# Nine TensorE products that nobody reads are taken out of a transformer tower

## The chip, the cores and the metric

One Trainium2 chip, of which the kernel uses one core, so nothing here goes between cores. A core has five engines that run their own lists of instructions side by side and wait for each other by semaphores: TensorE (PE: matrix products and transposes, written into eight banks of PSUM), VectorE (DVE), ScalarE (ACT), GpSimd (POOL) and SyncE (SP, which issues most DMAs). The metric is the time of one execution on the device in microseconds (us); smaller is better.

## The reference, cut to what matters

64 images are cut into 36 patches of 768 values each, embedded to 256 channels, and two more tokens are set in front. One attention-like layer and one feed-forward layer with 32 experts follow.

```
h = tokens(x) @ W_lin + b_lin (+ class token, positions)       # 64 x 38 x 256
h = h + attn(layernorm(h))     # up, 4-tap conv, q/k/v by blocks, gates,
                               # decayed scores, head norm, down
n = layernorm(h)
shared = silu(n @ gw) * (n @ uw) @ dw
e = argmax(n @ gate_w); s = sigmoid(max(n @ gate_w))
routed = silu(s*n @ G[e]) * (s*n @ U[e]) @ D[e]                # one of 32 experts
out = h + shared + routed
```

## The kernel before, in words

The work has two phases. In the first, eight groups of eight images (304 tokens, in three tiles of 114, 114 and 76 rows) go through everything but the experts. In the second the 32 experts are applied to the tokens that chose them, with weights of 1.5 MB for each expert read from memory.

The first phase is a software pipeline, written out by hand. `pipeline(pe, step)` (L1641) calls `step(e, f, a, m)` eight times: e is the group being embedded, f the group in the first layer norm, the products `up` and the convolution, a the group in attention, m the group in the second layer norm, the routing and the shared feed-forward. In the first steps a and m are None, and the list is short: this is the fill. After the eight steps the lists of the last groups are written out one after the other (L1643 to L1731): this is the drain. Each engine has such a list of its own. TensorE takes its list in order; where a step calls `pe.wait_ge`, everything behind it on TensorE waits too.

Names that the change and the prediction touch:

- `stream(bank, moving, times)` (L1345 to L1348) multiplies the identity by 512 columns of weights that lie in SBUF and writes them to a whole bank. It has no wait and increments no semaphore, and the next user of the bank starts it anew. It is called in six places for nine products in all.
- Fill, group 0, step 2: `h_rows_of` (L1364) transposes the tokens to rows, ACT copies them out (L505), DVE takes the statistics (L868, L872), POOL the reciprocal root (L442, L444), DVE normalises (`xn`, L878), and `to_columns` (L1381) transposes back. ACT and DVE split the result in a high and a low part (L505, L884), and the first of eight `up` products starts (L1390; each `up(f, k)` is six products and six records). `stream(ab[3], lin_w, 4)` stands ahead of `to_columns`, `stream(ab[3], lin_w, 1)` behind it.
- Between weight preparations: `merge_weights` (L1314 to L1321) multiplies small weight matrices, most with 8 columns. `turn_up` (L1331) transposes the `up` weights; DVE copies the two banks out (L831, semaphore `s_prep`); `mixed_gate_weights` (L1340) waits for `s_prep` at 20, which is the second copy, and makes 16 products of 8 columns. `stream(ab[3], lin_w, 1)` stands between `turn_up` and `mixed_gate_weights`. Then come `q_of` (L1416), `h_rows_of` and `scores` (L1455).
- Drain, last group in attention: ACT makes the decay factors (`cw`, L604), DVE weighs them (L950), and `heads(a, j)` (L1490) waits for tile j of them. `stream(fb[1], sd_w, 1)` stands ahead of `heads(a, 0)`. Behind the heads DVE makes the norm (L968 to L977), statistics (L984 to L999) and, after them in its list, `expert_act` (L1117), on which the second half of `gate_up(m, 1)` waits.
- Drain, last group in the shared layer: `ffn_rows` (L1364), `stream`, `to_columns` (L1381), `stream`, `route` (L1529 and L1532, which waits for the low part, L1060), `gate_up(m, 0)`. The second phase can start its products only behind this list (first ones at L2253).

Of the kernel before, what the change touches and what calls it, by code (L numbers as in the profile page):

```python
# [58 lines left out]
def groups_phase(nc, block, patches, w_lin, pos, cols, w_up, conv, chan, wq, wk, wv, wvt, w_gates, b_gates,  # L59
# [4 lines left out]
    fb, ab, mb = banks[0:2], banks[2:6], banks[6:8]  # L64

    with ExitStack() as ctx:
        def sb(name, shape, dt=f32):
            return ctx.enter_context(nc.sbuf_tensor(name, shape, dt))
# [21 lines left out]
        ident = sort.ident  # L90
# [5 lines left out]
        lin_w = sort.lin_w  # L96
# [4 lines left out]
        sd_w = sb("sd_w", [128, KI, D])  # L101
# [1205 lines left out]
        def _(pe):  # L1307
# [34 lines left out]
                last.then_inc(s_prep_mm, 1)  # L1342


            def stream(bank, moving, times):  # L1345
                for _ in range(times):
                    pe.matmul(bank[:, :], ident[:], moving[:, 0:2, :].rearrange("p k d -> p (k d)"),
                              start=True, stop=True)  # L1348

            def embed(f, c):  # L1350
                if c == 0:
                    pe.wait_ge(s_patch, 16 * f.n + 16)
                wait(pe, s_sz, KI * f.n - 1 + c)
                for k in range(KF):
                    last = pe.matmul(fb[c][:, 0:GS * N], lin_w[:, k, c * 128:(c + 1) * 128],  # L1355
                                     patch[:, k, :], start=(k == 0), stop=(k == KF - 1))
                last.then_inc(s_emb_mm, 1)
# [10 lines left out]
            def h_rows_of(f):  # L1368
                if f.n == 0:
                    pe.wait_ge(s_const, CONSTS)  # L1370
                pe.wait_ge(s_ht, KD * f.n + KD)
                to_rows(fb, h_t[:].rearrange("p c s t -> p c (s t)"), s_h_mm)

            def to_columns(dst, src, ready, n, done):

                for c in range(KD):
                    for j in range(NT):
                        if c == 0:
                            pe.wait_ge(ready, NT * n + j + 1)
                        rows = height(j)  # L1380
                        last = pe.transpose(dst[c][:, columns(j)], src[0:rows, j, c * 128:(c + 1) * 128],  # L1381
                                            ident[0:rows, 0:rows])
                    last.then_inc(done, 1)
# [11 lines left out]
            def up(f, k):  # L1395
                if f.n == 0:
                    pe.wait_ge(s_prep, 7 if k < KI else 8)
                if k < 2:
                    pe.wait_ge(s_xnl, KD * f.n + KD)
                elif k < 2 + KI:  # L1400
                    pe.wait_ge(s_xm, KI * f.n + k - 1)
                else:
                    pe.wait_ge(s_sz, KI * f.n + k - KI - 1)
                split_product(fb[k % 2][:, 0:GT], (up_hi, up_lo), (xn_hi, xn_lo), k * 128).then_inc(s_up_mm, 1)


            def q_of(a, heads_at):
                pe.wait_ge(s_xact, KI * a.n + KI)
                if a.n == 0:
                    pe.wait_ge(s_prep, 12)  # L1410
                for h in heads_at:
                    if h < 2:
                        wait(pe, s_att, KD * (a.n - 1) + h + 1)
                    else:
                        wait(pe, s_h2, 2 * a.n)
                    pe.matmul(ab[h][:, 0:GT], score_w[:, h], x_act[:, a.p, h, :],  # L1416
                              start=True, stop=True).then_inc(s_q_mm, 1)
# [4 lines left out]
            def v_of(a, j):  # L1422
                if a.n == 0:
                    pe.wait_ge(s_prep, 18)
                pe.wait_ge(s_ct, NT * a.n + j + 1)
                for h in range(NH):
                    last = pe.matmul(ab[j][0:height(j), h * 128:(h + 1) * 128], xm_tile(a, h, j), v_w[:, h],
                                     start=True, stop=True)
                last.then_inc(s_v_mm, 1)

            def mixed_gates(f):

                if f.n == 0:
                    bank = mb[0]
                    pe.wait_ge(s_prep, 22)
                else:
                    bank = fb[0]
                    pe.wait_ge(s_sz, KI * f.n + 1)
                for j in range(NT):
                    tile = columns(j)  # L1440
                    dst = bank[0:height(j), GT + 16 * j:GT + 16 * (j + 1)]
                    for c in range(KD):
                        pe.matmul(dst, xn_hi[:, c, tile], g_w[:, c], start=(c == 0), stop=False)
                    for c in range(KD):
                        last = pe.matmul(dst[:, 0:2 * NH], xn_lo[:, c, tile], g_w[:, c, 0:2 * NH],
                                         start=False, stop=(c == KD - 1))
                last.then_inc(s_gm_mm, 1)

            def scores(a, j):

                n, w = height(j), height(j) + 2 * NH
                if j == 0:
                    pe.wait_ge(s_q, NH * a.n + NH)
                for h in range(NH):
                    last = pe.matmul(ab[j][0:n, h * w:(h + 1) * w], x_act[:, a.p, h, columns(j)],  # L1455
                                     q_t[:, h, j, 0:w], start=True, stop=True)
                last.then_inc(s_c_mm, 1)

            def f_sums(a):
                pe.wait_ge(s_logf, a.n + 1)  # L1460
                pe.matmul(ab[3][0:R, 0:NT * NH], tri[:], logf[:].rearrange("p j h -> p (j h)"),
                          start=True, stop=True).then_inc(s_f_mm, 1)
# [113 lines left out]
            def ffn_rows(m):  # L1576
                pe.wait_ge(s_ffn, KD * m.n + KD)
                to_rows(mb, ffn_t, s_ft_mm)

            def step(e, f, a, m):  # L1580
                if a: q_of(a, range(1, NH))
                if f: h_rows_of(f)
                if a:
                    scores(a, 0)
                    scores(a, 1)
                    scores(a, 2)
                    if a.n == 0: mixed_gates(a)
                    v_of(a, 0)
                    v_of(a, 1)
                if f and f.n == 0: stream(ab[3], lin_w, 4)  # L1590
                if f: to_columns(fb, xn, s_xn, f.n, s_xnt_mm)
                if f and f.n == 0: stream(ab[3], lin_w, 1)
                if a: v_of(a, 2)
                if m: to_columns(mb, xn2, s_xn2, m.n, s_xn2t_mm)
                if f: up(f, 0)
                if a: f_sums(a)
                if f:
                    up(f, 1)
                    up(f, 2)
                if a: gates_t(a)  # L1600
                if f: up(f, 3)
                if f and f.n == 0: merge_weights()
                if m: route(m)
                if a:
                    tops_t(a)
                    decay(a, 0)
                    decay(a, 1)
                    decay(a, 2)
                if f: up(f, 4)
                if m: gate_up(m, 0)  # L1610
                if a:
                    heads(a, 0)
                    heads(a, 1)
                if a and a.n == 0:
                    heads(a, 2)
                if f: up(f, 5)
                if a and a.n > 0:
                    heads(a, 2)
                if m: gate_up(m, 1)
                if f:  # L1620
                    if f.n > 0: mixed_gates(f)
                    up(f, 6)
                if m:
                    ranks(m)
                    gate_up(m, 2)
                if m: gate_up(m, 3)
                if f: up(f, 7)
                if m: shared_down(m)
                if e: embed(e, 0)
                if m: ffn_rows(m)  # L1630
                if a: heads_t(a)
                if e: embed(e, 1)
                if f and f.n == 0:
                    turn_up()
                    stream(ab[3], lin_w, 1)
                    mixed_gate_weights()
                if a: down(a)
                if f: q_of(f, range(0, 1))
                if a: att_rows(a)

            pipeline(pe, step)  # L1641

            f, a, m = last, next_last, near  # L1643
# [54 lines left out]
            decay(a, 1)  # L1698
            route(m)
            decay(a, 2)  # L1700
            stream(fb[1], sd_w, 1)
            heads(a, 0)
            heads(a, 1)
            gate_up(m, 0)
# [10 lines left out]
            ffn_rows(m)  # L1715

            m = last
            stream(ab[1], sd_w, 1)
            to_columns(fb, xn2, s_xn2, m.n, s_xn2t_mm)
            stream(ab[1], sd_w, 1)  # L1720
            route(m)
            gate_up(m, 0)
            ranks(m)
# [649 lines left out]
```

## Time and profile before

| | us |
|---|---|
| median of 3 runs | 653.28 |
| lowest and highest | 651.33 and 653.66 |
| the profiled execution, own time | 654.7 |
| its span, first to last instruction | 652.9 |
| PE busy in the span | 607.6 (93%) |
| DVE busy | 429.5 (66%) |
| ACT busy | 375.2 (57%) |
| POOL busy | 197.4 (30%) |
| mean granted clock of TensorE | 0.988 of full speed |

The profile is one execution. Its times are from the start of the span. An engine is busy while it executes; a PE that is busy may still run at either of two clocks, 1.2 or 2.4 GHz, and the profile has the granted clock as a share of full speed. A product on fp32 data is two records of TensorE (the nine products are 18 records). Ends of products are modelled; their starts are measured. The chain of waits starts at the instruction that ended last and goes back, at each step, to what released it.

### The profile page before, as it was taken

The page shows a single profiled execution, that of the slowest core. Times are in us where ns is not written, and L with a number is a line of the kernel's source. Part 1 is how long each engine was busy: PE and PEld are TensorE (multiplying, and loading weights), DVE is VectorE, ACT ScalarE, POOL GpSimd, SP SyncE. Part 2 cuts the span into 40 slices and gives each one's busy share as a digit, 9 for nine tenths or more (in the row PEclk, how much of TensorE's full clock was granted, in tenths as well). Part 3 has the DMA queues.
Part 4 walks back from the last instruction along what each step waited for, and adds up shares of the span by engine and source line. Part 5 has one row for each costly group of instructions (what it writes and reads, how often), then busy time and mean ns, then how long its engine had stood idle before and what let it go on. Part 6 is the DMA issues. An engine that isn't in the chain of part 4 may idle for free.

```text
span 652.9 us, 10636 instructions
## 1 busy us (share of the span) xinstructions
PE 607.6 (93%) x3615; PEld 510.1 (78%) x3615; DVE 429.5 (66%) x1338; ACT 375.2 (57%) x839; POOL 197.4 (30%) x226
## 2 busy tenths in 40 slices
PE   4899899999998998999999998988999999999995
PEld 3688778878878878878878977766788888888884
DVE  1644785865856865866765866675876777776672
ACT  1328668449439529539538758243666666666661
POOL 5100110231232133133033233353256662232451
PEclk9999899999999999999998999899999999999999
DMA  8339410030030030030010011185999999999960
GB/s 291 132 85 369 122 56 1 20 94 21 20 95 21 20 94 21 19 95 21 8 51 20 2 37 37 35 303 169 392 391 378 379 348 350 373 369 404 343 214 23
DMA packets 44597, 101.56 MB, mean 156 GB/s; under 512 B 9295, under 2 KB 30589, under 8 KB 39672
## 3 DMA queue, kind: packets, MB, share of 16 engines
q1 hardware_dynamic: 35280, 89.07, 38.1%
q0 software_dynamic: 7696, 8.49, 4.7%
q10 hardware_dynamic: 1560, 3.23, 1.5%
q8 instruction: 32, 0.52, 0.4%
q14 instruction: 29, 0.24, 0.1%
HBM read 80.17 MB, written 23.32 MB: 159 GB/s over the span
## 4 chain that ended last, share of the span: by engine, by line
PE 71%; ACT 14%; DVE 8%; issue 2%; POOL 1%; DMA 1%; SPq 0%; DVEq 0%; ACTq 0%; POOLq 0%
PE bank L2253 16%; PE bank L1390 11%; PE bank L2272 9%; PE bank L1355 8%; PE bank L1512 4%; PE bank L1490 3%; PE bank L1455 3%; PE bank L2261 2%; PE bank L1416 2%; PE bank L1572 2%; PE bank L1364 2%; ACT v L505 2%; ACT hst L581 2%; ACT L596 1%; ACT L592 1%
## 5 line engine op out<-in xcount | busy, mean ns | idle before, releaser
L456 POOL TENSOR_TENSOR rstd_h<-var_h,minus_half 114x4 f32<-114x4 f32 (+1 forms) x24 | 24.3, 1014 | 173.3 <-DVE var_h L999 173.3
L2077 POOL DMA_INDIRECT out<-rows,bg x32 | 37.6, 1175 | 82.4 <-DVE rows L2143 81.1
L1355 PE MATMUL bank<-patch,lin_w 128*128 128x288 f32 x192 | 52.6, 428 | 8.7 <-DMA col_t<-cols 7.9
L2253 PE MATMUL bank<-w_hi,x_hi 128*128 128x512 f32 x148 | 56.5, 463 | 2.7 <-DVE x_lo L2155 2.7
L1355 PEld LDWEIGHTS bank<-patch,lin_w 128*128 128x128 f32 x192 | 37.4, 201 | 20.6 <-DMA col_t<-cols 7.9
L898 DVE SCALAR_TENSOR_TENSOR y<-xm,conv_t,y 128x296 f32<-128x296 f32 (+2 forms) x96 | 43.7, 512 | 6.2 <-ACT xm L505 6.2
L2253 PE MATMUL bank<-w_lo,x_hi 128*128 128x512 f32 x148 | 46.3, 394 | 0.0
L2253 PE MATMUL bank<-w_hi,x_lo 128*128 128x512 f32 x148 | 46.2, 393 | 0.0
L2179 DVE TENSOR_TENSOR act_e<-silu_e,bank 128x512 f32<-128x512 f32 x37 | 25.5, 688 | 31.0 <-PE bank L2253 30.3
L2149 DVE TENSOR_TENSOR w_lo<-wts,w_hi 128x1024 fp32r<-128x1024 f32 x36 | 43.1, 1217 | 0.5 <-ACT w_hi L2201 0.5
L2228 ACT ACTIVATE silu_e<-bank 128x512 f32<-128x512 f32 x37 | 22.1, 598 | 35.2 <-PE bank L2253 35.2
L1390 PE MATMUL bank<-xn_hi,up_hi 128*128 128x304 f32 x128 | 33.7, 346 | 6.0 <-ACT xm L505 4.9
L1841 POOL DMA_INDIRECT b_zone_dram<-base_rows,spot x24 | 31.1, 1295 | 26.9 <-DVE base_rows L1125 20.9
L505 ACT ACTIVATE att_t<-bank 128x304 f32<-128x304 f32 x15 | 6.3, 423 | 54.1 <-PE bank L1512 53.4
L2201 ACT ACTIVATE w_hi<-wts 128x1024 fp32r<-128x1024 f32 x36 | 36.8, 1049 | 0.0
L1841 POOL DMA_INDIRECT x_zone_dram<-xs_rows,spot x24 | 30.2, 1259 | 21.1 <-DVE spot L1103 9.0
L2196 ACT ACTIVATE x_hi<-bank 128x256 fp32r<-128x256 f32 x37 | 14.2, 383 | 38.9 <-PE bank L2242 28.1
L2143 DVE SCALAR_TENSOR_TENSOR rows<-bank,bg 128x256 f32<-128x256 f32 x37 | 15.7, 424 | 31.2 <-PE bank L2272 19.3
L1572 PE MATMUL bank<-act_t,sd_w 128*128 128x304 f32 x128 | 35.0, 424 | 1.2 <-DVE act_t L1117 1.2
L1390 PE MATMUL bank<-xn_hi,sgu_hi 128*128 128x304 f32 x128 | 31.6, 329 | 3.4 <-DVE act_t L1117 2.9
L1512 PE MATMUL bank<-hst,down_w 128*128 128x304 f32 x128 | 34.1, 420 | 0.1
L2272 PE MATMUL bank<-wts_down,act_et 128*128 128x256 f32 x144 | 34.1, 379 | 0.0
(261 smaller groups left out, 1658.8 us busy)
## 6 DMA issues: line engine op xcount, KB each, us to landing
wts<-w_exp SPq DMA_DIRECT2D x18, 1024.0 KB
x_act<-w_exp SPq DMA_DIRECT2D x10, 1024.0 KB
silu_z<-w_exp SPq DMA_DIRECT2D x9, 1024.0 KB
wts_down<-w_exp SPq DMA_DIRECT2D x18, 512.0 KB
patch<-patches SPq DMA_DIRECT2D x8, 864.0 KB, 6.0
down_w<-w_exp SPq DMA_DIRECT2D x10, 512.0 KB
lin_w<-w_exp SPq DMA_DIRECT2D x9, 512.0 KB
b_zone_dram<-act_t SPq DMA_DIRECT2D x1, 4160.0 KB, 28.4
```

The costliest lines, as they stand in the source:

```text
L898: dve.scalar_tensor_tensor(y[:, k, :, lag:], xm[:, f.p, k, :, 0:S - lag], w, y[:, k, :, lag:], ALU.mult, ALU.add).then_inc(s_conv, 1)
L1355: last = pe.matmul(fb[c][:, 0:GS * N], lin_w[:, k, c * 128:(c + 1) * 128], patch[:, k, :], start=(k == 0), stop=(k == KF - 1))
L1390: last = pe.matmul(dst, weights[w][:, c, at:at + 128], x[part][:, c, :], start=(n == 0), stop=(n == 3 * KD - 1))
L1512: last = pe.matmul(ab[c][:, 0:GT], down_w[:, k, c * 128:(c + 1) * 128], hst[:, k, :], start=(k == 0), stop=(k == KI - 1))
L1572: last = pe.matmul(mb[c][:, 0:GT], sd_w[:, k, c * 128:(c + 1) * 128], act_t[:, k, :], start=(k == 0), stop=(k == KI - 1))
L1841: pool.indirect_dma_start(zone, bass.IndirectOffsetOnAxis(ap=self.spot[0:n, t:t + 1], axis=0), rows[0:n, j, :], None, bounds_check=E * SLO ...
L2077: pool.indirect_dma_start(out, bass.IndirectOffsetOnAxis(ap=rows_at, axis=0), rows[:, k % 4, :], None, bounds_check=T - 1, oob_is_err=Fals ...
L2149: dve.tensor_tensor(w_lo[:, k % 2, u, :], wts[k % 4][:, u * KD * I:(u + 1) * KD * I], w_hi[:, k % 2, u, :].bitcast(f32), ALU.subtract).the ...
L2179: dve.tensor_tensor(act_e[:, e, :], silu_e[:, e, :], banks[3 + 2 * e][:, :], ALU.mult).then_inc(s_ae, 1)
L2201: act.activation(w_hi[:, k % 2, u, :], wts[k % 4][:, u * KD * I:(u + 1) * KD * I], ACT.Copy).then_inc(s_w_hi, 1)
L2253: last = pe.matmul(banks[2 + 2 * e + u][:, :], x[:, e, c * SLOT:(c + 1) * SLOT], w[:, e, u, c * I:(c + 1) * I], start=(n == 0), stop=(n == ...
L2272: last = pe.matmul(banks[6 + k % 2][:, 0:D], act_et[:, k % 2, c, :], wts_down[k % 4][:, c * D:(c + 1) * D], start=(c == 0), stop=(c == KI ...
```

## The change

All six calls of `stream` and the function itself are taken out. Nothing else is moved; the waits and the order of all other instructions stay.

```
-            def stream(bank, moving, times):
-                for _ in range(times):
-                    pe.matmul(bank[:, :], ident[:], moving[:, 0:2, :].rearrange("p k d -> p (k d)"),
-                              start=True, stop=True)
-
...
                     v_of(a, 0)
                     v_of(a, 1)
-                if f and f.n == 0: stream(ab[3], lin_w, 4)
                 if f: to_columns(fb, xn, s_xn, f.n, s_xnt_mm)
-                if f and f.n == 0: stream(ab[3], lin_w, 1)
                 if a: v_of(a, 2)
...
                 if f and f.n == 0:
                     turn_up()
-                    stream(ab[3], lin_w, 1)
                     mixed_gate_weights()
...
             route(m)
             decay(a, 2)
-            stream(fb[1], sd_w, 1)
             heads(a, 0)
...
             m = last
-            stream(ab[1], sd_w, 1)
             to_columns(fb, xn2, s_xn2, m.n, s_xn2t_mm)
-            stream(ab[1], sd_w, 1)
             route(m)
```

## Rows read from the trace of the kernel before

**Rows 1.** The page: span, engines' busy time, and granted clock in 40 slices.

```profile
span 652.9 us, 10636 instructions
...
PE 607.6 (93%) x3615; PEld 510.1 (78%) x3615; DVE 429.5 (66%) x1338; ACT 375.2 (57%) x839; POOL 197.4 (30%) x226
...
PEclk9999899999999999999998999899999999999999
```

**Rows 2.** The removed line by itself: ns min/median/max, first and last start in us.

```profile
L1347 PE MATMUL bank<-lin_w,ident x12: 592/592/644, 17.3 to 44.8; 128*128 128x512 f32 x12
...
L1347 PE MATMUL bank<-sd_w,ident x6: 592/594/676, 399.5 to 429.5; 128*128 128x512 f32 x6
```

**Rows 3.** The chain of waits: start us, length us, what.

```profile
7.93 8.10 PE bank L1355 x24
...
21.46 0.43 DVE xn L878
...
26.53 1.91 PE bank L1390 x12
...
31.91 4.99 PE bank L1390 x24
36.90 5.83 PE bank L1355 x24
...
44.47 0.91 PE bank L1347 x2
...
432.10 1.93 PE bank L1390 x12
...
436.95 3.65 PE bank L1390 x24
```

**Rows 4.** Timeline, first layer norm of the fill: start, length, idle before <-releaser.

```profile
17.33 3.60 PE L1347 MATMUL bank<-lin_w,ident 128*128 128x512 f32 x8
...
22.96 1.06 PE L1347 MATMUL bank<-lin_w,ident 128*128 128x512 f32 x2
24.35 0.52 PE L1390 MATMUL bank<-xn_hi,up_hi 128*128 128x304 f32 x2 [0.33 <-DVE xn_lo L884]
```

**Rows 5.** Timeline behind `turn_up`.

```profile
44.50 0.69 DVE L831 COPY x_act<-bank 128x512 f32<-128x512 f32 x1 [0.20 <-PE bank L1331]
45.25 1.95 PE L1340 MATMUL bank<-gm_w,x_act 128*128 128x8 f32 x16
```

**Rows 6.** Timeline, heads of the last group.

```profile
399.48 1.10 PE L1347 MATMUL bank<-sd_w,ident 128*128 128x512 f32 x2
399.82 0.63 DVE L950 TENSOR_TENSOR cw<-c_t,cw 114x456 f32<-114x456 f32 x1
...
400.42 1.91 PE L1490 MATMUL bank<-v,cw 114*114 114x128 f32 x16
...
403.20 0.16 DVE L968 COPY norm<-bank 114x4 f32<-114x4 f32 x1 [0.66 <-PE bank L1490]
```

**Rows 7.** Timeline, second layer norm of the last group.

```profile
426.52 1.02 PE L1347 MATMUL bank<-sd_w,ident 128*128 128x512 f32 x2
...
428.00 1.21 PE L1381 MATMUL bank<-ident,xn 114*128 114x114 f32 x6 [0.45 <-DVE xn L1054]
...
429.05 1.06 PE L1347 MATMUL bank<-sd_w,ident 128*128 128x512 f32 x2
...
430.35 0.39 PE L1529 MATMUL bank<-route_w,xn_hi 128*114 128x64 f32 x2 [0.24 <-DVE xn_lo L1060]
```

**Rows 8.** TensorE by stretch: length, PE busy (records), granted clock, DMA share, GB/s.

```profile
29.00:32.00 3.00, 3.00 (x29) 1.00 0.02 5
32.50:35.90 3.40, 3.40 (x16) 0.50 0.00 0
...
404.50:407.90 3.40, 1.24 (x10) 1.00 0.01 4
...
425.30:432.10 6.80, 5.06 (x28) 1.00 0.95 376
```

More of the change, by code:

```diff
@@ L1342, in mixed_gate_weights @@
                 last.then_inc(s_prep_mm, 1)
[L1345 to L1348, printed above, removed]
             def embed(f, c):
@@ L1589, in step @@
                     v_of(a, 1)
-                if f and f.n == 0: stream(ab[3], lin_w, 4)
                 if f: to_columns(fb, xn, s_xn, f.n, s_xnt_mm)
-                if f and f.n == 0: stream(ab[3], lin_w, 1)
                 if a: v_of(a, 2)
@@ L1634, in step @@
                     turn_up()
-                    stream(ab[3], lin_w, 1)
                     mixed_gate_weights()
@@ L1700, in _ @@
             decay(a, 2)
-            stream(fb[1], sd_w, 1)
             heads(a, 0)
@@ L1717, in _ @@
             m = last
-            stream(ab[1], sd_w, 1)
             to_columns(fb, xn2, s_xn2, m.n, s_xn2t_mm)
-            stream(ab[1], sd_w, 1)
             route(m)
```

## The prediction

> **What bounds the kernel now.** The page comes first. PE is busy 607.6 us of a span of 652.9 us, the next engine, DVE, 429.5 us [rows 1]: TensorE sets the pace. The row of granted clock shows four slices at 8 among the 9s [rows 1]: the clock is full nearly always and falls a few times for a moment. Next I looked at the removed line by itself: 12 records in the fill and 6 in the drain, 592 ns of modelled length each [rows 2], but two of them start to start with their neighbours take less: eight take 3.60 us [rows 4], 0.45 us for one, so a product of two records costs TensorE 0.9 us. Nine cost 8.1 us of its time. The chain of waits then says how much of this lies on the path, and the timeline what released the instruction behind each one. The last view is busy time and granted clock by stretch, since the nine products can do one thing besides costing time: keep the clock up.
>
> **What the removal gives back, place by place.**
>
> Layer norm of the fill, five products. The eight records at 17.33 end at 20.93, and the transposes behind them wait for DVE's xn, which starts at 21.46 [rows 3, 4]. The single product at 22.96 ends at 24.02, and the next instruction, at 24.35, was released by DVE xn_lo after an idle 0.33 us [rows 4]. Both lie in waits: 0.0 us.
>
> Behind `turn_up`, one product. The chain has it on the path with 0.91 us [rows 3], which looks like a gain. But `mixed_gate_weights` waits for the second copy of DVE, 44.50 + 0.69 = 45.19, and it starts at 45.25 [rows 5]. The copy is late next, at the same moment: 0.0 us, at most the 0.13 us by which the chain puts the end of the product at 45.38.
>
> Heads of the last group, one product, 399.48, or 0.94 us of TensorE between the last decay product and 400.42. `heads(a, 0)` could start at about 399.6, `heads(a, 1)` needs DVE's second weighing, 399.82 + 0.63 = 400.45, and is reached at about 400.5: no new wait. Who is late next is DVE: its norm at 403.20 idled 0.66 us for the heads [rows 6], and before that DVE had no gap. The chain runs from there through DVE to the next products, so the gain is 0.66 us at most of the 0.94; between 0 and 0.94 I take 0.6 us.
>
> Second layer norm of the last group, two products. 426.52 + 1.02 = 427.54, and the transposes start at 428.00, released by xn; 429.05 + 1.06 = 430.11, and `route` starts at 430.35, released by xn_lo [rows 7]. 0.0 us.
>
> So of 8.1 us of TensorE only 0.6 us come back. No semaphore, DMA or other engine's list is touched, and no wait is added.
>
> **What the clock takes.** Rows 8 have the key. From 29 to 32 PE is busy 3.00 of 3.00 us, but with products of 8 columns (29 records), and then the clock is at 0.50 (1.2 of 2.4 GHz) from 32.5 to 35.9. From 404.5 to 407.9 PE is busy only 1.24 us, waiting for DVE, and the next fall follows. From 425.3 to 432.1 the clock stays full, though the real work in it is 12 transposes and the small products of `route`; 1.02 + 1.06 us of its 5.06 busy us are the four wide records [rows 7, 8]. So the clock falls after a stretch in which few columns go through TensorE, by idling or by tiny products alike, and the nine products stand in just such stretches.
>
> The price of a fall, from rows at either level: 24 records of `up` take 4.99 us where most of them run low, and 24 of the same shape 3.65 us at full clock [rows 3]: 1.34 us. The other bound is a start from a cold engine: the first 24 records of the embedding take 8.10 us, the same 24 later 5.83 us: 2.27 us [rows 3] (the page prints a full clock there; the length of the records says otherwise). A low stretch of 3.4 us at half speed can cost at most 1.7 us; the cold start costs more because it lasts until enough dense work has gone through. After an idle engine I go by the second row, after a busy one by the first.
>
> Fill, layer norm. Without the five products PE has six transposes between 17.3 and 24.35. The clock is low when `up` starts: between 1.34 and 2.27 us, nearest to the cold start, 1.9 us. The 24 records of the four `up` run from 24.35 to 28.44 = 4.09 us where dense ones take 3.65, so 0.4 us is swallowed by waits for ACT. The transposes on the path run low too, +0.2 us (estimate: six in about 1 us, paced half by DVE). Against this stands the fall at 32.5: with `up` late, wide products fill part of the stretch ahead of the 8-column ones, and where this fall no longer comes 1.34 us return; I give it one in two, -0.7 us. Together 1.9 - 0.4 + 0.2 - 0.7 = +1.0 us, with bounds 0 and +2.5.
>
> Behind `turn_up`. From 44.4 to 47.1 only the 16 products of 8 columns are left, as between 29 and 32, and all behind them on the path (q_of, transposes, scores) is dense. A fall in nine of ten executions at 1.34: +1.2 us, with bounds 0 and 1.7.
>
> Heads of the last group. The product is replaced at once by the heads, which are dense. The wait behind them, which lets the clock fall already now [rows 8], stays. 0 us, between 0 and 0.5.
>
> Second layer norm of the last group. Without its two products 6.8 us go by with 12 transposes and the small products of `route`. `route` and `gate_up(m, 0)` (1.93 us for 12 records at full clock, rows 3) then run low, and the DVE chain that `gate_up(m, 1)` waits for starts later. Price between 1.34 and 2.27, and nearest to the cold start as the engine was idle first; plus nothing for the DVE wait, which hides part: +1.9 us.
>
> Sum: -0.6 + 1.0 + 1.2 + 0 + 1.9 = **+3.5 us**. On the profiled execution, 652.9 us of span and 1.8 us around it, 654.7 us, this gives 658.2 us. That execution lies 1.4 us above the median of 653.28, about one fall more than the median run may have had. I add the difference to the median: 653.3 + 3.5 = **656.8 us**. Behind each place the chain goes on mostly through TensorE, so I let nothing swallow a delay later.
>
> A rule of the Trainium skill ("TensorE: Matmul & The Clock Gate", section "Why this matters for your kernels") asks only that TensorE have no long idle gaps between bursts of matmuls to avoid drops in the middle of a kernel. The row 29 to 32 disagrees: no gap, and the clock fell [rows 8]. By that rule the place behind `turn_up` would keep its clock, which is the second rival below.
>
> **The rivals.**
>
> No fall. The clock stays up at all three places, because the transposes and small products that are left suffice. For it: the granted clock is full in most of the first phase in spite of many waits of about a microsecond. Against it: two falls of rows 8 after stretches no emptier. It then gives only the heads' 0.6 us, perhaps 0.9 with the copy: 652.4 to 652.7 us, not slower. It decides from the point at which the 12 transposes in 425.3 to 432.1 hold the clock by themselves. Chance 0.15.
>
> Idle alone counts. The clock falls in the two layer norms, but not behind `turn_up`, where PE's records lie nearly without a gap. -0.6 + 1.0 + 1.9 = +2.3: 655.6 us. Chance 0.12. Rows 8 (29 to 32) speak against it.
>
> Longer falls. Low clock makes the stretch behind it emptier in columns, so one fall brings the next, and the old fall at 32.5 stays. Upper bounds: 2.5 + 1.7 + 0.5 + 2.27 = 7.0, less 0.6: 659.7 us. For it: the cold start costs 2.27 and not 1.34. Against: each fall in the trace ends after one stretch of 3.4 us [rows 8]. Chance 0.13.
>
> **How the numbers follow.** The forecast has 0.60, with 655.0 to 659.0 us of its own (falls depend on where they meet the work, which differs from run to run). The measurement can tell about 0.5%, here 3.3 us: above 656.5 is slower, below 650.0 faster. Of the forecast 0.44 lies above 656.5 and 0.16 below; of idle alone 0.02 and 0.10; of longer falls 0.12 and 0.01; no fall gives 0.10 within and 0.05 faster (if more than the 0.94 us of the heads' place comes back). Slower 0.58, same 0.37, faster 0.05. The range leaves out no fall at its lower end and the last bit above: 653.5 to 660.3 us.
>
> **What would show it.** In the profile after: granted clock 0.50 at about 24 to 28, while the first `up` run; 0.50 for some 3.4 us between 45 and 52; 0.50 at 430 to 436. Starts: the first `up` still at about 24.4 to 24.8, `mixed_gate_weights` right behind DVE's copy, DVE's norm behind the heads without its 0.66 us of idle. The embedding that now starts at 36.9 should start within 0 to 2.5 us later. I would be wrong if the clock is 1.00 in the second layer norm of the last group, or if the low stretches are there and the end isn't later, which would mean a wait that I have not seen swallows them.

## The result and the profile after

| | before | after |
|---|---|---|
| median, 20 runs each | 653.35 us | 657.51 us |
| lowest to highest | 650.86 to 656.73 | 652.96 to 661.03 |
| ratio, 95% interval | | 1.0055 [1.0035, 1.0076] |
| profiled execution: time, span | 654.7, 652.9 | 658.1, 656.3 |

The changed kernel is slower by 0.55%, 3.6 us by the ratio and 4.2 us by the medians. 656.8 us were forecast.

The page of the changed kernel shows a PE that is busy 2.5 us less in a span 3.4 us longer, though 8.1 us of products are gone, and two slices at 6 and 8 in the fill where [rows 1] had 9s:

```profile
span 656.3 us, 10600 instructions
...
PE 605.1 (92%) x3597; PEld 511.0 (78%) x3597; DVE 429.5 (65%) x1338; ACT 375.5 (57%) x839; POOL 197.2 (30%) x226
...
PEclk9698899999999999999999999979999999999999
```

TensorE by stretch in the changed kernel (length, PE busy and records, granted clock, DMA share, GB/s). All three stretches are low from end to end, one for each place of which I had forecast a fall. In the second PE is busy for the whole 6.60 us:

```profile
19.60:29.60 10.00, 6.26 (x25) 0.50 0.21 89
46.90:53.50 6.60, 6.60 (x21) 0.50 1.04 361
...
432.60:439.20 6.60, 6.09 (x30) 0.50 1.00 349
```

The chain of waits of the changed kernel (start, length, what). Line numbers are 5 lower from L1350 on (L1385 is `up` and `gate_up`, L1350 the embedding, L1411 `q_of`):

```profile
7.89 8.43 PE bank L1350 x24
...
24.88 5.77 PE bank L1385 x24
...
34.12 3.63 PE bank L1385 x24
...
37.82 6.06 PE bank L1350 x24
...
45.65 0.70 DVE x_act L831
...
46.40 3.27 PE bank L1340 x16
49.67 4.16 PE bank L1411 x8
...
434.47 3.41 PE bank L1385 x12
...
440.94 3.63 PE bank L1385 x24
```

The same chain before, behind the removed product of `turn_up` (`mixed_gate_weights`, `q_of`, the transposes of `h_rows_of`):

```profile
45.38 1.83 PE bank L1340 x16
47.20 2.15 PE bank L1416 x8
49.35 0.66 PE bank L1364 x6
```

Read against [rows 3 to 5, 7]:

- Fill. The first 24 `up` products take 5.77 us; before they ran from 24.35 to 28.44, 4.09 us. The next 24 take 3.63 us and not 4.99, because the old fall at 32.5 did not come. The second embedding starts at 37.82 and not 36.90; 0.3 us of this were there before the first removed product (the first embedding ends at 16.32, before 16.03). The place costs 0.6 us in this trace.
- Behind `turn_up`. `mixed_gate_weights` starts right behind DVE's copy, 45.65 + 0.70, as forecast, so nothing is gained. Then its 16 products take 3.27 us (before 1.83 in the chain) and `q_of` 4.16 (before 2.15). From the start of the second embedding to the end of `q_of` it is 16.01 us, before 36.90 to 49.35 = 12.45: the place costs 3.6 us. About 0.2 us of it is the embedding itself (6.06 us for 5.83), which the trace of `m_fill` below shows too, with the product in place.
- Last layer norm. From the start of `route` to the start of the last 24 `gate_up` products: 432.07 to 440.94 = 8.87 us, before 430.35 to 436.95 = 6.60. The place costs 2.3 us.

At the heads both norms of DVE now follow each other without the 0.66 us of idle of [rows 6]. The timeline of the changed kernel has them in one row, with no idle time ahead of it:

```profile
405.37 0.22 DVE L968 COPY norm<-bank 114x4 f32<-114x4 f32 x2
```

In this execution two falls of the kernel before, at 353 and 408 us, did not come. At the 1.34 us of the prediction for each, that hides about 2.7 us (an estimate) of what the three places cost.

The runs carry their own granted clock, which makes the cause countable. Of the 20 runs of the changed kernel the fastest has 652.96 us at a clock of 0.986 (span 651.1), the longest 661.03 at 0.971 (659.2). Low time is twice the missing clock times the span: 18 and 38 us. A line through all 20 runs has 0.44 us of time for 1 us of low clock (correlation 0.94), 1.5 us for a low stretch of 3.4 us; I had taken 1.34 from [rows 3].

### The profile page after: what moved, and what is told of

Read it like the earlier page. It is cut to its first block, busy times and chain, and to the rows that moved or that the text cites. A ratio compares the mean times of both kernels' runs of the same rounds, so it can differ in the third digit from the quotient of the medians.

```text
span 656.3 us, 10600 instructions
## 1 busy us (share of the span) xinstructions
PE 605.1 (92%) x3597; PEld 511.0 (78%) x3597; DVE 429.5 (65%) x1338; ACT 375.5 (57%) x839; POOL 197.2 (30%) x226
## 4 chain that ended last, share of the span: by engine, by line
PE 70%; ACT 15%; DVE 9%; issue 3%; POOL 1%; DMA 1%; SPq 0%; DVEq 0%; ACTq 0%; POOLq 0%
PE bank L2242 16%; PE bank L1385 10%; PE bank L2261 9%; PE bank L1350 8%; PE bank L1507 4%; PE bank L1411 3%; PE bank L1450 3%; PE bank L2250 2%; PE bank L1567 2%; PE bank L1485 2%; PE bank L1359 2%; ACT hst L581 2%; ACT cw L604 2%; ACT v L505 2%; ACT L596 1%
## 5 line engine op out<-in xcount | busy, mean ns | idle before, releaser
L1350 PE MATMUL bank<-patch,lin_w 128*128 128x288 f32 x192 | 52.6, 428 | 8.7 <-DMA col_t<-cols 7.9
L1350 PEld LDWEIGHTS bank<-patch,lin_w 128*128 128x128 f32 x192 | 37.4, 201 | 20.8 <-DMA col_t<-cols 7.9
L1385 PE MATMUL bank<-xn_hi,up_hi 128*128 128x304 f32 x128 | 33.9, 348 | 6.5 <-ACT xm L505 4.6
L1385 PE MATMUL bank<-xn_hi,sgu_hi 128*128 128x304 f32 x128 | 32.0, 332 | 3.3 <-DVE act_t L1117 2.4
```

Of the source, the lines that this page charges most:

```text
L1385: last = pe.matmul(dst, weights[w][:, c, at:at + 128], x[part][:, c, :], start=(n == 0), stop=(n == 3 * KD - 1))
```

## The experiments

Ratios are against the kernel before on the same chip in the same session, whose median was 650.6, 651.8, 652.3 and 651.7 us in the four sessions. One execution of each kernel was profiled. The removed products are named by place: fill (five), turn (one, behind `turn_up`), heads (one), last (two). In most edits a line below stands for a call put back or taken out.

**One place put back, the rest removed: `r1_fill`, `r2_turn`, `r3_last`.**

```
r1_fill:  + if f and f.n == 0: stream(ab[3], lin_w, 4)   and   stream(ab[3], lin_w, 1)
r2_turn:  + stream(ab[3], lin_w, 1)      # between turn_up() and mixed_gate_weights()
r3_last:  + stream(ab[1], sd_w, 1)       # twice, around to_columns of the last group
```

> The changed kernel with the five products of the first layer norm put back. Theory (the clock, place by place): the low stretch around the first up products is gone, the fall inside or behind the 8-column products of merge_weights is back in about half of the executions, the long low stretch behind turn_up and the one in the last layer norm stay. Against the kernel before: -0.6 (heads) + 3.5 or 1.2 (turn_up, as the changed kernel's trace or as my prediction has it) + 2.0 (last) = 2.6 to 4.9 us slower. Rival (where the falls land is chance, and the place of a product does not matter): between 0 and 4 us slower, with low stretches at the first up products too.

> The changed kernel with the one product between turn_up and mixed_gate_weights put back. Theory: no fall behind turn_up; the fill is low from about 19 to 30 and the last layer norm at 432 to 439. Against the kernel before: -0.6 + 0.6 to 1.0 (fill) + 2.0 (last) = 2.0 to 2.4 us slower, that is 1.2 to 3.5 us less than the changed kernel loses. Rival (idle time alone brings the clock down, one product between two busy stretches does nothing): 4 us slower, like the changed kernel.

> The changed kernel with the two products of the last layer norm put back. Theory: full clock from 425 to 440; against the kernel before -0.6 + 0.6 to 1.0 + 1.2 to 3.5 = 1.2 to 3.9 us slower, 2 us less than the changed kernel loses. Rival (the DVE chain behind route hides the low clock there): 4 us slower, as the changed kernel.

Measured: r1_fill 657.53 us, ratio 1.0107 [1.0055, 1.0159] (6 runs); r2_turn 654.76 us, 1.0052 [1.0028, 1.0075] (12 runs); r3_last 656.01 us, 1.0066 [1.0033, 1.0100] (12 runs). By the ratios, these are losses of 7.0, 3.4 and 4.3 us, each more than was expected (2.6 to 4.9, 2.0 to 2.4 and 1.2 to 3.9).

The clock by stretch answers by place. The same stretches, first of r1_fill, then r2_turn, then r3_last:

```profile
19.60:29.60 10.00, 8.20 (x41) 1.00 0.27 112
46.90:53.50 6.60, 6.60 (x35) 0.74 1.04 359
...
432.60:439.20 6.60, 5.40 (x30) 0.68 0.87 310
```

```profile
19.60:29.60 10.00, 6.74 (x29) 0.54 0.19 79
46.90:53.50 6.60, 6.60 (x54) 1.00 1.03 359
...
428.50:432.40 3.90, 3.05 (x15) 0.50 1.00 338
```

```profile
19.60:29.60 10.00, 7.29 (x34) 0.66 0.21 89
46.90:53.50 6.60, 6.60 (x55) 1.00 1.05 373
...
432.60:439.20 6.60, 5.82 (x35) 1.00 0.61 226
```

Wherever products were put back, that place runs at 1.00; where they were not, it is low for at least a part of the stretch, but for the turn place of r3_last. (A share between 0.50 and 1.00 is a window that the low time fills only in part.)

The profiled executions of all fourteen runs of this document give the same answer. The fill place is low in all five without its products (changed kernel, a_again, r2_turn, r3_last, m_fill) and in one of nine with them (b1_start, below). The turn place is low in five of the six without its 512-column product (changed kernel, a_again, r1_fill, m_turn, s1_tiny; not r3_last) and in none of eight with it. The last place is low, for 6.8 us each time, in all four without its products and in none of ten with them. So the products of a place guard that place.

The times follow less cleanly: each kernel loses 3.4 to 7 us, and r1_fill lost no less than the changed kernel. The intervals, 1.5 us on each side for r2_turn and 3.4 us for r1_fill, hardly separate the three.

**One place taken out, the rest kept: `m_fill`, `m_turn`, `r4_noheads`.**

```
m_fill:     - stream(ab[3], lin_w, 4)   and   - stream(ab[3], lin_w, 1)   # layer norm of the fill
m_turn:     - stream(ab[3], lin_w, 1)   # behind turn_up()
r4_noheads: - stream(fb[1], sd_w, 1)    # ahead of heads(a, 0)
```

> The kernel before without the five products of the first layer norm, all others kept. Theory: low clock while the four first up products run (from about 20 to 28 or 30), which costs 1.5 to 2.2 us up to merge_weights; the fall behind merge_weights then comes in fewer executions and gives 0.7 to 1.3 back: 0.5 to 1.5 us slower in the median. Rival (r1_fill, which kept the five, was no faster than the changed kernel: the two falls cancel): 0 us.

> The kernel before without the one product between turn_up and mixed_gate_weights, all others kept. Theory (after the traces of the changed kernel and of s1_tiny: two low stretches in a row, since the 8-column products at low clock leave the next stretch as empty): 3 to 3.5 us slower in executions in which it comes, which is most: 2.5 to 3.5 us in the median. Rival (my first sizing, one stretch of 3.4 us): 1.2 us.

> The kernel before without the product ahead of the heads of the last group; all others stay. Theory: DVE's norm no longer idles for the heads (0.66 us before), the last weighing of DVE is late next, no new fall: 0.6 us faster than before, 0.1%, at the edge of what five rounds show. Rival 1: the decay factors of ACT set the chain there anyway, 0.0 us. Rival 2: the stretch from 396 to 400 is then too empty and the clock falls in some executions: 0.5 to 1 us slower.

Measured, 12 runs each: m_fill 652.72 us, 1.0010 [0.9992, 1.0028], 0.7 us; m_turn 657.51 us, 1.0069 [1.0036, 1.0102], 4.5 us (2.3 to 6.6); r4_noheads 651.03 us, 0.9999 [0.9966, 1.0031], which tells neither a gain of 0.6 us nor none.

The chain of m_fill has the cancelling pair of the fill again: the first 24 `up` long, the second 24 short. The second embedding starts at 36.88, before 36.90, so in this execution the two cancel altogether.

```profile
24.14 5.56 PE bank L1390 x24
...
33.17 3.63 PE bank L1390 x24
...
36.88 6.06 PE bank L1355 x24
```

The chain of m_turn has one low stretch behind `turn_up` in its profiled execution, with `q_of` (L1416) at 3.38 us. The scores (L1455) start 15.02 us after the second embedding's start at 36.24, before 50.01 - 36.90 = 13.11 us: 1.9 us for the one stretch, the 0.2 us of the embedding among them. The 16 products of 8 columns ran ahead of the fall, 44.82 to 46.77, at full speed. A second view, by stretch, has a fall of 10 us much later, in the drain, where the profiled execution of the kernel before had one of 3.4 us:

```profile
44.82 1.95 PE bank L1340 x16
46.77 3.38 PE bank L1416 x8
50.15 1.10 PE bank L1364 x6
51.26 2.25 PE bank L1455 x24
```

```profile
355.00:365.00 10.00, 10.00 (x51) 0.50 0.01 3
```

PE is busy for all of these 10 us, with the decay products, `route` and heads, at 0.50. So a low clock can last far longer than the 3.4 us that I had priced. That the edit, 300 us earlier, made this fall long isn't shown: the kernel before, in the same session, had executions of up to 657.61 us at a clock of 0.984, the clock of this execution too.

In r4_noheads no fall came at all until the last products, a span of 649.2 us, and DVE's norms follow without idling. From DVE's second weighing (L950) to the start of `expert_act` (L1117) behind the norms it is 398.03 to 404.90 = 6.87 us, before 399.82 to 407.45 = 7.63: here the product's removal gives back 0.76 us. Up to the heads this kernel's lists are those of the kernel before, and yet the falls at 32.5, 73 and 353 us did not come. Falls come and go from one execution to the next:

```profile
0.00:640.00 640.00, 600.70 (x3605) 1.00 0.46 158
```

```profile
400.60 0.22 DVE L968 COPY norm<-bank 114x4 f32<-114x4 f32 x2
```

**The changed kernel again: `a_again`.** No edit.

> The changed kernel again, beside the three that put one place back, in more executions. Theory: its loss is the sum of three places and is larger than that of each of the three: at least 4.1 us, the median of the first comparison, and more than r2_turn's 4.1 us by 1 to 3.5 us if the fall behind turn_up comes in most executions. Rival (the places don't add up, the loss is where the falls happen to land): about the same as r2_turn, 4 us.

Measured: 659.51 us, 1.0084 [1.0049, 1.0120] (10 runs), 5.5 us. Its profiled execution is low at the same three places, it has the fall of the kernel before at 353 (here at 359), and not the one at 408. Its ratio is above that of r2_turn by 0.3%, but the intervals overlap.

**Columns or idle time: `s1_tiny`.** The 512-column product of the turn place is replaced by four of 8 columns.

```
-                    stream(ab[3], lin_w, 1)
+                    tiny(ab[3], lin_w, 4)   # pe.matmul(bank[:, 0:8], ident[:], moving[:, 0, 0:8])
```

> The kernel before with the one 512-column product between turn_up and mixed_gate_weights replaced by four products of 8 columns, which keep TensorE busy for about as long (8 records at 0.11 us, 0.9 us). Theory (few columns bring the clock down, busy or not): low clock for 3.4 to 7 us somewhere from 45 to 54, as in the changed kernel, and 1.2 to 3.5 us slower than before. Rival (only idling brings it down): full clock from 42 to 54 and the time of before within 0.5 us.

Measured: 656.67 us, 1.0086 [1.0053, 1.0118] (7 runs), 5.6 us, more than the 1.2 to 3.5 expected. TensorE by stretch, then its timeline (L1352 is `tiny`, L1420 is `q_of`):

```profile
45.90:52.80 6.90, 6.90 (x24) 0.52 1.05 365
```

```profile
44.02 1.00 PE L1352 MATMUL bank<-lin_w,ident 128*128 128x8 f32 x8
44.97 2.89 PE L1340 MATMUL bank<-gm_w,x_act 128*128 128x8 f32 x16
47.71 4.40 PE L1420 MATMUL bank<-x_act,score_w 128*128 128x304 f32 x8
```

The small products take 0.95 us from start to start, where the wide one took 0.91, and leave PE no gap, and the clock is low for nearly all of the 6.90 us. Idle time is not needed for a fall; that rival is out. The rule on long idle gaps of the Trainium skill ("TensorE: Matmul & The Clock Gate", section "Why this matters for your kernels") names one cause of two here: in the fill of the changed kernel PE was idle for 4.43 us ahead of `to_columns`, at 22.23, and the clock was low from 19.6 on; behind `turn_up` there is no such gap.

**Unread products where the kernel before still has falls: `b2_cover` (and `b2_again`).**

```
-            stream(fb[1], sd_w, 1)                          # heads
+    if u and k == 1 and m.n == G - 2: stream(fb[1], sd_w, 2)   # in gate_up, wait at 406
+    if f.n == 1: stream(mb[1], lin_w, 1)                       # ahead of mixed_gates, 70.5
+    narrow(ab[3], lin_w); narrow(ab[0], lin_w) twice           # 256 columns each, 351 to 353
+    pe.wait_ge(s_v, NT * a.n + 1)                              # ahead of the second narrow
```

> The kernel before without the product at the heads, and with unread products in three other waits of TensorE where the clock falls before: one of 512 columns before the mixed gates of group 1 (70.5 us), three of 256 columns in the waits from 351 to 353, two of 512 columns in the wait for DVE at 406 to 408. Theory: the falls at 73, 353 and 408 are gone; each came in most executions at 1.3 us, the products cost 0.1 to 0.5 us of path: 2 to 3 us faster than before, and fewer slow executions. Rival (the waits there hide the low clock, or the products push the path): 0 to 1 us slower.

> The kernel b2_cover a second time, since its gain of 0.16% lay at the edge of its interval. Theory: with the falls at 73, 353 and 408 us covered the slow executions (above 653) are missing; the median is 0.5 to 1 us below before. Rival (no gain): ratio 1.000 with as many slow executions as before.

Measured, 12 runs each: 651.04 us, 0.9984 [0.9968, 1.0000], and 650.81 us, 0.9975 [0.9949, 1.0000]. The highest of the 24 runs is 652.31 us, while the kernel before reached 656.95 and 657.48 beside them. Three stretches of b2_cover and, behind it, of the kernel before:

```profile
69.00:77.00 8.00, 7.98 (x50) 1.00 0.31 92
349.00:357.00 8.00, 8.00 (x64) 1.00 0.16 41
404.00:412.00 8.00, 7.25 (x47) 1.00 0.01 2
```

```profile
69.00:77.00 8.00, 7.13 (x42) 0.79 0.32 93
349.00:357.00 8.00, 6.74 (x41) 0.79 0.16 41
404.00:412.00 8.00, 5.77 (x35) 0.79 0.03 8
```

The falls are gone, and the spread is smaller. The gain is 1.0 and 1.6 us by the ratios and not 2 to 3, with both intervals reaching to 1.0000. r4_noheads shows in part why: the kernel before doesn't have these falls in every execution.

**A warm start: `b1_start`, `b4_both`.**

```
b1_start: + pe.wait_ge(s_warm, 1)              # DVE sets the tile warm to 1.0 first
          + for _ in range(14): pe.matmul(ab[3][:, :], warm[:, 0:128], warm[:, :], ...)
            pe.wait_ge(s_w_emb, 3 * 16)
b4_both:  b1_start + b2_cover, and
-                if f and f.n == 0: stream(ab[3], lin_w, 4)
+                if f and f.n == 0: stream(ab[3], lin_w, 6)
```

> The kernel before with 14 products of 512 bf16 columns on a constant tile at the very start, while TensorE waits for the first weights and patches (0 to 7.9 us); nobody reads them. Theory: the embedding starts at the same 7.9 us at full clock and takes about 5.9 us and not 8.1. Of these 2.2 us ACT's split of the up weights (14.5 to 16.5, ahead of its copy at 17.3) takes back all but about 0.8 us: 0.8 us faster in all. Rival 1: the clock isn't what makes the first 24 records long (the loads beside them are): no change, embedding still 8.1 us. Rival 2: the whole 2.2 us come through.

> b2_cover with the 14 products at the start, and 6 products and not 4 in the first layer norm, since the embedding then ends 2 us earlier and the wait for ACT is longer. Theory (in b1_start the earlier end left an empty stretch from 14 to 16.5 and brought a low clock at 24.5 to 28, which ate the 0.8 us): the first up starts at 23.5 at full clock, no fall before 32; 0.8 us faster than b2_cover, 1.3 to 1.8 us faster than before. Rival: the wait from 14 to 16.5 itself brings the fall whatever follows, and it is as b1_start with the cover, 0 to 1 us slower than b2_cover.

Measured, 12 runs each: b1_start 653.01 us, 1.0030 [1.0005, 1.0056]; b4_both 648.87 us, 0.9957 [0.9930, 0.9985]. The timeline of b1_start and its clock in the first `up`, then the same of b4_both (L1353 is `stream`, L1361 the embedding, L1387 and L1390 `to_columns`):

```profile
7.84 6.09 PE L1361 MATMUL bank<-patch,lin_w 128*128 128x288 f32 x24 [0.67 <-DMA col_t<-cols]
...
15.24 3.60 PE L1353 MATMUL bank<-lin_w,ident 128*128 128x512 f32 x8
21.10 1.19 PE L1387 MATMUL bank<-ident,xn 114*128 114x114 f32 x6 [2.26 <-DVE xn L881]
```

```profile
24.50:27.90 3.40, 3.30 (x16) 0.63 0.00 0
```

```profile
15.06 5.32 PE L1353 MATMUL bank<-lin_w,ident 128*128 128x512 f32 x12
21.05 1.19 PE L1390 MATMUL bank<-ident,xn 114*128 114x114 f32 x6 [0.67 <-DVE xn L881]
```

```profile
24.50:27.90 3.40, 3.13 (x24) 1.00 0.02 5
```

The embedding takes 6.09 us where it took 8.08: by the length of its records the start had been at low clock. In b1_start the products of the layer norm then end 2.26 us before xn, and the clock is low while the first `up` run. Instead of 0.8 us faster the kernel came out 0.3% slower, 2 us. Its trace doesn't show that loss: the old fall at 32.5 didn't come in this execution, and the second embedding starts at 36.21, 0.7 us earlier than in the trace before. Why the runs are slower stays open.

With two products more the idle time ahead of xn is 0.67 us and the `up` run at full clock. b4_both is 3.5 us below the median of before beside it (2.8 by the ratio, 1.3 to 1.8 expected), and 1.9 us below b2_again in the same session. The 2.0 us less of embedding come through only as 0.9 us of earlier `up` (23.47 against 24.35), since ACT's split of the weights ends at 16.5 in any case.

## Why the prediction was right

What comes back: right at each place. Nothing in the fill, nothing behind `turn_up` (DVE's copy is late next, as the chain now shows), nothing in the last layer norm. At the heads DVE's idle 0.66 us is gone as forecast, and its chain is 0.76 us shorter in the trace of r4_noheads; that this reaches the end wasn't resolved (±2 us).

The clock falls at the three places: right, and shown by place. Each fall goes when the place's own products are put back, and `s1_tiny` shows that it comes behind products of 8 columns with no idling at all.

The fill, +1.0: 0.6 us in the trace of the changed kernel, nothing in that of m_fill, 0.7 us (-0.5 to 1.8) in the runs of m_fill. The cancelling with the old fall at 32.5 is in both chains (5.77 and 3.63; 5.56 and 3.63).

Behind `turn_up`, +1.2, bounds 0 and 1.7: this term was mis-sized, and its upper bound too. It measured 3.6 us in the trace of the changed kernel, 1.9 us in that of m_turn, and 4.5 us (2.3 to 6.6) in the runs of m_turn, part of which may be falls elsewhere. I had priced one stretch of 3.4 us of dense products. But where the fall meets the 16 products of 8 columns, they take 3.27 us for 1.83, the clock stays low, and `q_of` runs low behind them (4.16 us for 2.15). The five traces that have this fall divide by that. In the changed kernel, a_again and s1_tiny the small products ran at low clock (starts at 46.40, 47.47 and 45.03, falls at 46.8, 48.3 and 45.8), and it lasted 6.8 us. In m_turn and r1_fill they were over, or nearly so, when it came (ends at 46.77 and 48.41, falls at 47.5 and 47.7), and it lasted 3.4 us.

My third rival, longer falls, named this; I gave it 0.13 for all places together, on the ground that every fall of the trace before ended after one stretch. [Rows 8] print only the one at 32.5; two others of that view are

```profile
353.40:356.80 3.40, 3.40 (x16) 0.51 0.06 17
...
408.00:411.30 3.30, 3.30 (x15) 0.50 0.02 5
```

In all of them much of what ran at low clock were wide products (`up`, `gate_up`, decay), and in none of them the 8-column ones.

The last layer norm, +1.9: 2.3 us in the trace. Sized by the cold start, which was the nearer row.

Why the sum still came out, 3.5 against 3.6 to 4.2: in part by luck. The terms of the trace, 0.6 + 3.6 + 2.3 - 0.6 = 5.9 us, are more than the medians show in the first comparison and near the 5.5 us of a_again. The turn term was 2.4 us too small, and in the profiled execution two falls of the kernel before, at 353 and 408 us, were missing, which hides about as much. Such falls come and go (r4_noheads); whether the changed kernel also has them less often, because its list stands elsewhere when it comes to them, stays open. Nor do the single places add up: 0.7 and 4.5 us with about 2 for the last place would make 7 us, and with the turn product kept r2_turn still loses 3.4 us. How much of m_turn's 4.5 us is its place, and how much is falls such as the one of 10 us in its drain, was not measured.

## What to carry to other kernels

An unread product in a wait cost nothing here where its end lay before the release of the next instruction; read that in the timeline, not in the chain, which had put 0.91 us of the turn product on the path that were not there to gain. Ask of every wait and of every run of small products what stands behind it: one wide product of 0.9 us kept 3.6 us behind `turn_up`, two kept 2.3 us in the last layer norm, and five in the fill kept 0 to 0.6 us. When such a product goes, don't price the fall by one stretch alone: look at what it will meet. Here it lasted 3.4 us where the 8-column products were already over and 6.8 us where it met them. And compare profiles of more than one execution, since falls come and go.

## What was not expected of the hardware

One product of 512 columns (0.9 us) decides over 6.6 us and more of low clock (46.9 to 53.5 at 0.50, PE busy throughout), and four of 8 columns in its place do not help. A low clock lasted 10 us while PE was busy 10.00 of 10.00 us (m_turn, 355 to 365). Run to run the time of one kernel moves by 6 to 8 us with the granted clock (652.96 us at 0.986, 661.03 at 0.971); the covered kernel, with fewer falls, also spread less, 2.6 us over 24 runs (649.70 to 652.31).
